# A two-layer graph network kernel: the products with the count matrix in whole float32 instead of float32r high and low parts

## The reference: what is computed

```python
h  = relu(layernorm(x))
# layer 0
msg = (h[src] + edge_attr) @ Wm.T + bm
agg = segment_sum(msg, dst) / max(deg, 1)
out = h + gelu(concat(h, agg) @ Wu.T + bu)
x   = x + layernorm(out) * gamma + beta
# layer 1
h   = relu(layernorm(x))
rst = (1 + eps) * h + segment_sum(h[src], dst)
x   = x + relu(rst @ W1 + b1) @ W2 + b2 + h
```

## Time and profile before

| | |
|---|---|
| median of 3 runs | 487.54 us (486.55 to 487.87) |
| the profiled execution, its time | 488.46 us |
| its span | 486.7 us |
| PE busy | 471.4 us, 97% of the span |
| DVE, ACT, POOL busy | 266.0, 165.5, 120.6 us |
| chain that ended last, share of PE | 82% |
| mean granted TensorE clock | 0.996 of full |

### The profile page before, as it was taken

How to read it: one execution, slowest core, us unless ns; L and a number is a source line. 1 busy time by engine, 2 the same in 40 slices (tenths; PEclk the granted TensorE clock), 3 DMA queues, 4 the chain that set the end, 5 groups by cost and what they waited for, 6 DMA issues and landing times.

```text
span 486.7 us, 9356 instructions
## 1 busy us (share of the span) xinstructions
PE 471.4 (97%) x3297; PEld 281.4 (58%) x3297; DVE 266.0 (55%) x614; ACT 165.5 (34%) x312; POOL 120.6 (25%) x185
## 2 busy tenths in 40 slices
PE   7999999999999999999999999899999999999997
PEld 5545545455545456777766655799744449444442
DVE  4798886778787878876958699923000000011011
ACT  6677642333333338412047287620012213000000
POOL 4016343443344331000001113249980000000000
PEclk9999999999999999989999999999999999999999
DMA  8999999999999999996330111040230000010111
GB/s 283 382 396 408 408 386 373 403 392 406 401 373 393 407 404 398 369 349 237 147 105 23 43 43 40 5 170 1 56 118 0 0 0 1 22 43 23 43 43 38
DMA packets 31720, 98.92 MB, mean 203 GB/s; under 512 B 3672, under 2 KB 4696, under 8 KB 31674
## 3 DMA queue, kind: packets, MB, share of 16 engines
q1 hardware_dynamic: 30458, 97.27, 52.9%
q10 hardware_dynamic: 1216, 1.05, 0.7%
HBM read 95.76 MB, written 2.56 MB: 202 GB/s over the span
## 4 chain that ended last, share of the span: by engine, by line
PE 82%; DVE 8%; issue 4%; DMA 2%; DVEq 1%; POOL 1%; ACT 1%; SPq 0%; POOLq 0%
PE ps L1452 14%; PE ps L1437 14%; PE ps L1170 11%; PE ps L1218 6%; PE ps L1189 6%; PE ps L1384 4%; PE ps L1198 4%; PE ps L1279 4%; PE ps L1360 3%; PE ps L1280 3%; PE ps L1361 3%; PE ps L1122 3%; PE ps L1178 2%; DMA WmN<-in_L_gnn_Wm_dram 1%; DVE acc L790 1%
## 5 line engine op out<-in xcount | busy, mean ns | idle before, releaser
L438 POOL TENSOR_TENSOR aggT<-turned_sums,aggT 128x88 f32 x118 | 61.0, 517 | 97.3 <-ACT turned_sums L511 84.3
L746 DVE TENSOR_TENSOR A<-ps,A 128x220 f32 x158 | 60.7, 384 | 33.1 <-PE ps L1189 24.2
L1088 DVE TENSOR_TENSOR U<-ps,U 128x512 f32<-128x512 f32 (+1 forms) x10 | 6.9, 692 | 128.5 <-PE ps L1452 128.5
L1452 PE MATMUL ps<-W2s,hid 128*128 128x512 f32 (+1 forms) x160 | 68.8, 592 | 0.0
L1437 PE MATMUL ps<-aggT,W1s 128*128 (+1 forms) x192 | 67.3, 513 | 0.0
L1170 PE MATMUL ps<-ea,oneD 128*22 128x256 f32 x944 | 62.6, 383 | 3.2 <-issue 2.2
L1437 PEld LDWEIGHTS ps<-aggT,W1s 128*128 128x128 f32 x192 | 36.4, 190 | 30.7 <-issue 30.6
L1170 PEld LDWEIGHTS ps<-ea,oneD 128*22 128x22 f32 x944 | 23.3, 101 | 50.1 <-issue 26.3
L1452 PEld LDWEIGHTS ps<-W2s,hid 128*128 128x128 f32 (+1 forms) x160 | 30.0, 188 | 38.2 <-issue 38.2
L505 ACT COPY packed_sums<-ps 128x256 f32<-128x256 f32 x59 | 22.0, 372 | 80.9 <-PE ps L1170 80.7
L1360 PE MATMUL ps<-AR,Hh 128*128 128x256 f32 (+2 forms) x160 | 44.0, 311 | 0.7 <-DVE Hl L1055 0.7
(11 more groups left out here) (149 smaller groups left out, 651.8 us busy)
## 6 DMA issues: line engine op xcount, KB each, us to landing
ea<-in_edge_attr_dram SPq DMA_DIRECT2D x78, 1024.0 KB, 8.7
X<-in_x_dram SPq DMA_DIRECT2D x1, 2304.0 KB
xt<-in_x_dram SPq DMA_DIRECT2D x9, 256.0 KB, 3.6
out_dram<-U SPq DMA_DIRECT2D x9, 256.0 KB
W1s<-in_L_gnn_W_dram SPq DMA_DIRECT2D x1, 2048.0 KB, 9.0
W2s<-in_L_gnn_W_dram SPq DMA_DIRECT2D x1, 2048.0 KB, 8.3
Wu2N<-in_L_gnn_Wu_dram ACTq DMA_DIRECT2D x2, 512.0 KB, 4.4
WmN<-in_L_gnn_Wm_dram SPq DMA_DIRECT2D x1, 1024.0 KB, 7.2
```

What stands on the lines that cost most here:

```text
L438: nc.gpsimd.tensor_tensor(cols, sums, cols, ALU.add).then_inc(early_step, 1)
L746: V.tensor_tensor(cols, ps[:, 4 + m % 2, half * KW:(half + 1) * KW].rearrange("p (h w) -> p h w", w=W), cols, ALU.add).then_inc(add_step, 1)
L1452: last = T.matmul(ps[0:rows, 6 + b % 2, :], hid[:, k, b * P:b * P + rows], W2s[:, k, :], start=k == 0, stop=k == KC - 1)
```

## The change

`h` and `A` enter the products as float32. `Hh` and `Hl` are gone, with the casts, the subtractions and the waits for them; each block takes one matmul instead of two. The path for large counts is gone on all engines, with `most` and its transposition. `degree_products` is cut in two halves of five matmuls, in the pairs that hold steps 68 and 70, and `degrees` is read at step 72 instead of 69; the additions of a bias (`add_bias`) move to steps 62 to 72, those of `has_bias` to 74 to 78. POOL's addition of `h` at the end takes one operation per tile instead of two.

```diff
-    X, x_at = place("X", [P, NT, D], F32)
-    Hl, _ = place("Hl", [P, NT, D], F32R, x_at)
-    Hh, hh_at = place("Hh", [P, NT, D], F32R)
+    X, _ = place("X", [P, NT, D], F32)
...
-    ARc, arc_at = place("ARc", [P, NT, 512], F32R)
-    ARd, _ = place("ARd", [P, NT, 256], F32R, arc_at + NT * 256 * 4)
-    AR, _ = place("AR", [P, NT, NP], F32R, stream_at)
+    ARc, arc_at = place("ARc", [P, NT, 512], F32)
+    ARd, _ = place("ARd", [P, NT, 256], F32, arc_at + NT * 256 * 4)
+    AR, _ = place("AR", [P, NT, NP], F32, stream_at)
...
-    DEG_AT = FOLD_AT[-1] + 3
+    DEG_AT = FOLD_AT[-1] + 2
+    DEG_PARTS = [range(0, NT // 2), range(NT // 2, NT)]
...
-    BIAS_AT = [n for n in range(DEG_AT - 2, DEG_AT + NT - 1) if n != OUT_AT]
-    HAS_AT = [min(OUT_AT + 1 + b, NG - (NT - b + 1) // 2) for b in range(NT)]
+    BIAS_AT = [n for n in range(EARLY + 3, EARLY + NT + 4) if n != OUT_AT]
+    HAS_AT = [NG - (NT - b + 1) // 2 for b in range(NT)]
...
             def piece(i):
...
-                    pe.wait_ge(low0_ready, c + 1)
+                    pe.wait_ge(h0_ready, c + 1)
...
-                    T.matmul(to, Hh[:, c, rows], here, start=c == 0 and (q < 2 or f % 2 == 0), stop=False)
-                    last = T.matmul(to, Hl[:, c, rows], here, start=False, stop=c == NT - 1 and (q < 2 or f % 2 == 1))
+                    last = T.matmul(to, X[:, c, rows], here, start=c == 0 and (q < 2 or f % 2 == 0), stop=c == NT - 1 and (q < 2 or f % 2 == 1))
...
             def times_A(b, chunk):
-                pe.wait_ge(split1, b + 1)
+                pe.wait_ge(h1_ready, b + 1)
...
-                    T.matmul(to, Hh[:, b, rows], AR[:, b, start:start + cols], start=b == 0 and (cols == 512 or f % 2 == 0), stop=False)
-                    last = T.matmul(to, Hl[:, b, rows], AR[:, b, start:start + cols], start=False, stop=b == NT - 1 and (cols == 512 or f % 2 == 1))
+                    last = T.matmul(to, X[:, b, rows], AR[:, b, start:start + cols], start=b == 0 and (cols == 512 or f % 2 == 0),
+                                    stop=b == NT - 1 and (cols == 512 or f % 2 == 1))
...
-            def degree_products():
-                pe.wait_ge(fold_step, HB)
-                T.transpose(ps[0:1, DEG_BANK, 256:256 + P], most[:], ident[:])
-                for d in range(NT):
+            def degree_products(part):
+                pe.wait_ge(fold_step, HB - 1)
+                for d in part:
...
-                if DEG_AT - 1 in pair:
-                    degree_products()
+                for part, at_step in zip(DEG_PARTS, (DEG_AT, DEG_AT + 2)):
+                    if at_step in pair:
+                        degree_products(part)
...
-                for work, lag in ((gelu, 0), (h1, 3), (h1_high, 3), (h1T, 3)):
+                for work, lag in ((gelu, 0), (h1, 3), (h1T, 3)):
...
-                     (x1_moments2, 2), (o_variance, 1), (x1_variance, 2), (low_h1, 4)]
-            for k in range(NT + 5):
+                     (x1_moments2, 2), (o_variance, 1), (x1_variance, 2)]
+            for k in range(NT + 4):
```

More of the change, by code:

```diff
@@ L6 @@
 F32 = mybir.dt.float32
-F32R = mybir.dt.float32r
 BF16 = mybir.dt.bfloat16
@@ L23 @@
 EPS = 1e-5
-COUNT_MAX = 4096
 PREP_FIRSTS = 3
@@ L50, in gnn_kernel @@
     LAST = N - QS[-1][0]
-    XW = 256
-    NX = NP // XW
     WU_ORDER = list(range(FC, 2 * FC)) + list(range(FC))
     assert ETAIL % 2 == 0 and ETAIL <= GE // 2 and D == GE and FC == 4 and sum(n for _, n in QS) == NP
-    assert len(QS) == 3 and QS[2][1] * 2 == 512 and KW <= 256 and NT == 10
+    assert len(QS) == 3 and QS[2][1] * 2 == 512 and KW <= 256 and NT == 10 and E < 1 << 16
     EAGER = FC - 1
@@ L69, in gnn_kernel @@
     U_AT = [QUARTERS[b * FC:(b + 1) * FC] for b in range(NT)]
-    HH_AT = [FULL + b for b in range(NT)]
     ASIDE = {LATE_PRODUCT_AT[0]: ("product", EAGER), BIAS_PRODUCT_AT[0]: ("product", FC)} | {n: ("wu1", j) for j, n in enumerate(WU1_AT)}
@@ L121, in gnn_kernel @@
     Wu1N, _ = place("Wu1N", [P, FC, D], F32, u_at)
[L122 to L126, removed]
+    WmN, _ = place("WmN", [P, FC, D], F32, first_at)
+    Wu2T, _ = place("Wu2T", [P, FC, D], F32, first_at + 8192)
+    bm_parts, _ = place("bm_parts", [P, D], F32, first_at + 16384)
+    bmB, _ = place("bmB", [P, FC, QUAD], F32, first_at + 18432)
+    onesP, _ = place("onesP", [P, P], F32, first_at + 18944)
     acc, _ = place("acc", [P, NP], U16, w1_at)
@@ L298, in gnn_kernel @@
         small_in = sem("small_in")
-        split1 = sem("split1")
         stored = sem("stored")
@@ L384, in _ @@
             sp.dma_start(b2B[:], b2.rearrange("(a d) -> a d", a=1).broadcast_to([P, D])).then_inc(late_in, 16)
-            sp.wait_ge(most_ready, 2)
+            sp.wait_ge(deg_mm, 2)
             def load_x(b):
@@ L598, in _ @@
                 piece_conv(i)
-            act.wait_ge(most_ready, 2)
-            large = act.value_load(most1[0:1, 0:1], min_val=0, max_val=E + P)
             act.wait_ge(sum_step, 2 * (NG - EARLY))
             act.wait_ge(piece_mm, 2 * NT)
[L603 to L607, removed]
             def full_conv(c):
@@ L792, in degrees @@
             def degrees():
[L793 to L796, removed]
+                dve.wait_ge(deg_mm, 2)
                 V.tensor_scalar(degs[:], ps[:, DEG_BANK, 384:384 + NT], 1.0, None, ALU.max).then_inc(deg_step, 1)
@@ L894, in _ @@
                     bias_out()
-                for b in range(NT):
-                    if HH_AT[b] == n:
-                        low_h0(b)
                 for c in range(1, HB):
@@ L900, in _ @@
                         fold(c)
[L901 to L904, removed]
+                if n == DEG_AT + 4:
                     degrees()
@@ L969, in _ @@
             dve.wait_ge(agg_done, 2 * FC)
[L971 to L988, removed]
-            large = dve.value_load(most1[0:1, 0:1], min_val=0, max_val=E + P)
-            with dve.If(large > COUNT_MAX):
-                dve.wait_ge(extra_conv, 1)
-                extra(0)
             def packed(first):
@@ L1080, in _ @@
             dve.wait_ge(rst_done, 4)
-            with dve.If(large > COUNT_MAX):
-                extra(1)
-            V.nop().then_inc(past_large, 1)
             for b in range(NT):
                 dve.wait_ge(y_mm, b + 1)
-                dve.wait_ge(res_step, 3 * b + 3)
+                dve.wait_ge(res_step, 2 * b + 2)
                 rows = P if b < NT - 1 else TAIL
@@ L1333, in _ @@
                 piece(i)
-            def extra(layer):
-                done = layer * NX * NT
-                with pe.Fori(0, NX) as q:
-                    with pe.Fori(0, NT) as c:
-                        pe.wait_ge(extra_ready, q * NT + c + (done + 1))
-                        for f in range(FC):
-                            to, rows = ps[:, CHUNK_BANK[f], 0:XW], slice(f * P, (f + 1) * P)
-                            T.matmul(to, parts[:, 0, rows], rest[:, 0:XW], start=True, stop=False)
-                            last = T.matmul(to, parts[:, 1, rows], rest[:, 0:XW], start=False, stop=True)
-                        last.then_inc(extra_mm, 1)
-                        pe.wait_ge(extra_add, q * NT + c + (done + 1))
-            pe.wait_ge(most_ready, 2)
-            large = pe.value_load(most1[0:1, 0:1], min_val=0, max_val=E + P)
-            with pe.If(large > COUNT_MAX):
-                pe.wait_ge(sum_step, 2 * (NG - EARLY))
-                pe.wait_ge(agg_done, 2 * FC)
-                extra(0)
             def times_A(b, chunk):
-                pe.wait_ge(split1, b + 1)
+                pe.wait_ge(h1_ready, b + 1)
                 pe.wait_ge(conv, b + 1)
@@ L1424, in _ @@
             last.then_inc(rst_mm, 1)
-            with pe.If(large > COUNT_MAX):
-                pe.wait_ge(rst_done, 4)
-                extra(1)
             pe.wait_ge(w1_in, 16)
```

44 lines of the change are left out of this document (5 added, 39 removed).

## The result

| | before | after |
|---|---|---|
| median | 487.71 us (4 runs, 486.55 to 488.02) | 557.74 us (4 runs, 557.53 to 557.81) |
| ratio | | 1.144, 95% interval 1.142 to 1.146 |
| profiled execution, its span | 488.46, 486.7 us | 557.74, 556.0 us |

The change costs 70.0 us by the medians and 69.3 us between the two profiled executions. The forecast was 67.4 us more, 554.9 us, with a range of 551 to 560; the measured time lies in it, and 0.7 us above the narrower 552.5 to 557 that had been given 73%.

The account below looks back on a forecast made before the run. TensorE, busy 97% of the span, was taken as the bound. Terms 77.2 - 4.4 - 1.1 - 2.5 - 1.8 = +67.4 us on 487.5 gave 554.9 us; range 551 to 560, narrower 552.5 to 557 at 73%.

Parts of the forecast that it names:

- Price of a matmul: Products with A in both layers: one float32 matmul replaces two float32r ones at nearly twice their joint time, +77.2 us.
- 256 columns: Layer 1 matmuls of that width: price set at 0.438 us between 0.388 and 0.861, +16.9 us for 80.
- The gaps of float32r: Ends of each run of pieces: 0.2 us lost passing between float32r and float32; 4.4 of 5.0 us come back.
- Waits: TensorE's waits for low parts and one-hots in the loop give back 1.1 us, those of the third stage 2.5.
- ScalarE's cycle: Third stage, transposed tile's copy to next h1, 4.4 us: TensorE waits 0.6 us at the second tile.
- Clock: Behind the ten one-column matmuls: halves with pieces between avoid the fall to half clock, -1.7 us.
- That the clock falls after a half: Rival, behind the degrees: clock falls after one or both halves, +1.7 to +3.4 us, 556.6 to 558.3; 12%.
- That a wait comes between: Rival: ScalarE's cycle, loads of x or dearer matmuls on 256 columns add 8 us, about 562; 8%.
- That a float32 matmul is one record: Rival, all products with A: one record per matmul instead of two, kernel at about 470 us; 1.5%.
- That part of the second matmul was hidden: Rival, mainly second and third stage: they absorb more, so -3 to -6 us, 549 to 552; 5%.
- The moved additions of VectorE: In the loop: they stay hidden, VectorE being busy 49 of 62 us while the stage grows by 27.
- the residual of POOL: Fourth stage, ahead of the output layer: 24 us of work, now a third shorter, stays hidden.

Follow-up runs that it names:

- kernels 1 and 2: The kernel before with whole float32 in layer 0's product alone (523.92 us, ratio 1.0737), and in layer 1's product alone (522.18 us, ratio 1.0718).
- kernel 6: The kernel before without the path for large counts and with the degrees in halves, h still split; 485.86 us, ratio 0.996.
- Kernels 7: The kernel before without the matmuls on the low part of h, casts, subtractions and waits kept; 468.51 us, ratio 0.9613.
- kernel 8: kernel 6 with the low part of h left out altogether, subtractions and their waits too; 456.89 us, ratio 0.9353 to the kernel before.
- experiment 4: The changed kernel with the ten one-column matmuls of the degrees in one run again; 558.57 us, where the halves gave 557.74.
- kernels 3: The kernel before with the degrees in two halves, read three steps later, and the additions of has_bias moved behind that; 486.46 us, ratio 0.9972.

## Why the prediction was right, and what in it was not

**Price of a matmul: right.** 0.467 to 0.861 on 512 columns, 0.227 to 0.430 on 256 and 0.225 to 0.381 on 226 are the cause; kernels 1 and 2 add up to the change. **256 columns** were bounded by 0.388 and 0.861 and set to 0.438 by a straight line. Measured, a chunk A and one of B take 5.16 us in the chain of the changed kernel, A alone 3.44, so four matmuls on 256 cost 1.72, one 0.430: 0.6 us less in all. On 226 sixteen records take 3.05 us, 0.381 a matmul instead of 0.388: 0.5 less.

```profile
310.42 3.05 PE ps L1191 x16
...
340.35 3.44 PE ps L1253 x8
344.22 5.16 PE ps L1253 x16
```

**The gaps of float32r: wrong.** This is the step that failed: "Each passage between float32r and float32 leaves a gap", 4.4 us to come back. Only 0.2 us did. The timeline of the changed kernel, single steps and then a pair:

```profile
190.75 1.07 PE L1091 MATMUL ps<-ea,oneD 128*22 128x128 f32 x32
191.75 3.70 PE L1191 MATMUL ps<-ARc,X 128*128 128x512 f32 x8
195.38 1.07 PE L1091 MATMUL ps<-ea,oneD 128*22 128x128 f32 x32
...
206.53 7.13 PE L1191 MATMUL ps<-ARc,X 128*128 128x512 f32 x16
213.59 1.95 PE L1091 MATMUL ps<-ea,oneD 128*22 128x128 f32 x64
```

From 191.75 to 195.38 there are 3.63 us for eight records that take 3.44; from 206.53 to 213.59 there are 7.06 for sixteen that take 6.88. So 0.19 and 0.18 us are left for each run, short or long, with float32 on both sides, where it was 0.20. The change of type costs next to nothing. What changes at both ends is the shape: the sums write 22 rows of PSUM from 22 columns of the array, the pieces use all of it. That this is the cause is argued, not tested. Where both sides used the whole array, the kernel before had no gap to give back, though the types differ. Between two tiles of `map_agg` (float32) with `late` pieces (float32r) there are 6.12 us, and eight records at 0.430 and 24 matmuls at 0.112 are 6.13:

```profile
261.62 3.60 PE L1384 MATMUL ps<-CT,aggT 128*128 128x512 f32 x8
...
267.74 3.60 PE L1384 MATMUL ps<-CT,aggT 128*128 128x512 f32 x8
```

Around the transpositions nothing came back either: the transpositions take 0.44 us to the next matmul in the changed kernel (325.14 to 325.58), and in the kernel before 0.36 to the first of float32r and 0.09 more between this and the second:

```profile
325.14 0.60 PE L1262 MATMUL ps<-ident,X 128*128 128x128 f32 x4
325.58 3.60 PE L1253 MATMUL ps<-AR,X 128*128 128x512 f32 x8
```

So of the 4.4 us only 12 x 0.02 came back, in the loop. With the measured prices, this gap, and the waits at their idle time, the sum is 77.2 - 1.1 (the two prices) - 0.2 - 1.1 - 2.7 - 1.8 = +70.3, where the profiles show 69.3.

**Waits: right in place, somewhat small in size.** The first piece starts at 187.15, 0.5 earlier, the wait of 0.47 is gone, and the 3.1 us of the third stage became 0.43, at the place that the forecast gave for ScalarE's cycle, the second tile (0.6 expected):

```profile
317.78 0.66 PE L1262 MATMUL ps<-ident,X 128*128 128x128 f32 x4 [0.43 <-ACT X L587]
```

That wait was there before, with the same 0.43; the other four are gone:

```profile
283.54 0.65 PE L1369 MATMUL ps<-ident,X 128*128 128x128 f32 x4 [0.43 <-ACT X L625]
```

A wait costs more than the idle time printed beside it, since that is counted only from the end of the last matmul's duration (279.51 + 3.60 = 283.11 us), which overlaps with what follows where matmuls are back to back. From 279.51 to 283.54 there are 4.03 us, and eight records take 3.44: 0.59 lost, not 0.43. Counted so, from start to start, the third stage gave back about 3.4 us instead of 2.5, and the loop 1.7 instead of 1.1 (0.5 at the first piece; 0.66 at the sums ahead of the degrees, with 2.54 us from 211.09 to 213.63 where kernel 6 takes 1.88; 0.5 at two other pairs of sums). These 1.3 us over the 1.1 and 2.7 above bring the sum to 69.0. The forecast's 67.4 thus came near because errors cancelled in part: 4.2 us too much for the gaps, against 1.1 too much in the prices and about 1.5 too little for the waits.

**Clock: right in size, and for the right reason, but read as a fixed cost.** The profiled execution of before had one fall (1.7 us). The runs have none, one or two, and the medians of before (487.5 to 488.0) are those of runs with one; the changed kernel has none in four runs. The Trainium skill (TensorE: Matmul & The Clock Gate, "HAM oscillation — how this bites in real kernels") puts falls of the clock down to TensorE waiting between bursts of matmuls. Kernels 7 and 8 agree, with waits and a mean clock of 0.973 to 0.996; experiment 4 differs, since TensorE was busy 4.50 of 4.50 us before the fall, with narrow work.

**The rivals.** That the clock falls after a half: refuted by four runs of the changed kernel, and by 12 each of kernels 3 and 6. Its 556.6 to 558.3 us hold the measured 557.74 all the same, so the time alone would have pointed at the wrong cause; the clock of 1.00 tells them apart. That a wait comes between: 0.43 us of it, no more. That a float32 matmul is one record: refuted by the counts. That part of the second matmul was hidden: refuted by 1 and 2, but for the waits. The moved additions of VectorE cost nothing: TensorE is busy 90.30 of 90.35 us in the loop. Nor does the residual of POOL cost anything that shows: from the hidden layer to the end there are 139.8 us, and 139.4 before. No run tests either by itself.

## What to carry to other kernels

Where TensorE is the bound, a float32 product is priced by its records: one float32 matmul is two records, each of which takes nearly twice as long as a float32r matmul (0.430 against 0.233 us on 512 columns). Splitting one operand in two float32r parts is the cheaper way where the other operand needs no split, as the counts here, and where another engine has room for the work. Were both to be split, an estimate from the same 0.233 is 0.70 us for three matmuls and 0.93 for four, against 0.861. Read the distance between starts, not durations, and keep a gap apart from its cause until something on one side of it changes. A change that bundles a loss with small gains should be taken apart: the degrees in halves and the dropped path gave 0.4% (485.86 us) once the float32 was left out.

## What the runs showed of the hardware that I had not expected

- The granted clock can fall behind a stretch of work without any wait: in experiment 4 it fell in three of six runs behind two steps' sums on 22 columns of the array and ten one-column matmuls; with five of them behind the same sums it fell in none of 28 runs (kernels 3 and 6 and the changed one). With five, but with waits of TensorE ahead of them, it fell again (kernel 8). One fall costs 1.7 us, and one kernel shows three distinct times (486.4, 488.0, 489.6).
- A run of full matmuls between narrow ones loses 0.18 to 0.20 us, for float32r and float32, for 8 and for 16 records. Passages between the two types on the whole array lose nothing that shows (6.12 us for 6.13 of matmuls).
- An idle time of 0.43 us in the profile stood for 0.59 us lost between the starts of matmuls.
- A float32 matmul on 226 to 512 columns takes 1.68 ns a column (0.381 and 0.861 us), a float32r one on 226 and 256 columns 0.112 and 0.113 us, no less for fewer columns.
